# A hybrid block (linear attention, routed experts, state-space scan) in fp32: a third buffer of transposed rows, convolution products moved into the batch ahead, and a new slot table

## Chip, cores, metric

One core of one Trainium2 chip runs the whole block as one program. The metric is device microseconds of one execution, lower is better. The engines are TensorE (PE, its weight loads PEld), VectorE (DVE), ScalarE (ACT), GpSimd (POOL) and SyncE (SP, which here only issues DMAs).

## What is computed

`x` has 8 sequences ("batches") of 512 rows of 256 floats. Three residual blocks follow each other, each on a layer-normalised input:

```
x = x + attention(norm(x))      # 16 heads, linear: feature map elu+1
x = x + experts(norm(x))        # router, top 1 of 8, 256 -> 512 -> 256
x = x + ssm(norm(x))
ssm: xz = x @ in_proj.T;  xc, z = split(xz)           # 512 channels each
     u  = causal conv over 4 taps, full 512 x 512 channels, + bias
     dt = clip(sigmoid(u @ dt_w.T + dt_b));  B, C = u @ B_w.T, u @ C_w.T
     for t: state = exp(-dt*exp(A_log)) * state + dt*B*u + 1e-6   # 16 states
            y = sum_n(state * C) + D*u
     out = (y * silu(z)) @ out_w.T
x = x + experts(norm(x))        # the same experts again
```

The line above shows the order of the calls in the kernel: attention, experts, state-space block, experts.

## The kernel before

Everything is fp32 and stays in SBUF where it fits: 128 partitions, x as 32 chunks of 128 rows. The program has five stages: attention over the 8 batches (to about 210 us), experts (to about 395 us), a preparation for the scan (to 462 us), the scan stage (to 1254 us), experts again. Every engine has its own instruction list, and they wait for each other by counting semaphores.

**The scan stage** takes most of the time. Each batch is 64 **slots**, q = 0 to 63: state n = q // 4 of the 16 states, channel block k = q % 4 of the four blocks of 128 channels. In every slot

- ACT makes the decay `exp(dt*a)` of three slots later into one of five tiles (`m_decay`, L781) and one 128 x 512 quarter of the scaled input of the next state (`m_input`, L791);
- PE turns the scaled input from time-major to channel-major by four transposes into one of three PSUM banks (`m_spread`, L1366, which is the line of the helper `turned` for all transposes of this kind);
- DVE runs the recurrence over 512 times as one scan instruction (`m_scan`, L1241), which needs the decay and the bank.

After the four scans of a state POOL multiplies the 128 x 2048 result by that state's row of C (`c_product`, L530; SP has broadcast the row from DRAM into one of two tiles, L417), and adds it by an accumulating DMA onto the state two before (`add_on`, L539): two chains, of even and of odd states. States 0 and 1 start the chains. One ring of seven tiles (`m_h`) holds the scanned states; two of the seven lie in the upper half of `x`.

Between these fixed parts hangs all the other work, and **the table of slot numbers** at the top of the file tells in which slot of its engine each piece stands; it is the order within each engine's list and no clock time. For the *next* batch: 32 convolution products on PE (`m_conv`, L1668, at `CONV_AT`: four outputs of eight products), copy of u out of PSUM on ACT (`UC_AT`, L729), its transposes (`UT_AT`, L1676), B and C (`BC_AT`, L1685), dt (`DT_AT`, L1699), its tanh, clip and transposes, the weighing with dt on DVE (`WT_AT`). For the batch in hand: the gate z (`Z_AT`, L1730, and `ZTH_AT`, `GATE_AT`, L1183). For the batch *before*: skip terms on ACT (`SKIP_AT`, L772), sums of the two chains on DVE (`ADD_AT`, L1191 and L1198), the product with the gate (`FINAL_AT`, L1203), output products (`OUT_AT`, L1741), the update of x (`UPDATE_AT`, L1212) and row statistics. For the batch *after the next*: the norm of its rows on POOL (`m_norm`, L523, behind the products of the states in `NORM_AFTER`), its transposes on PE (`XT_AT`) and their copy on ACT into one of two buffers `m_xt` (`m_xtcopy`, L723, at `XTC_AT`). At slots 59, 61 and 62 PE also multiplies constants into a bank that nobody reads (`m_spin`, L1802).

The norm writes two chunks at a time into `m_xn`, which shares its memory with `m_bc` (B and C of the next batch), and so waits until C is stored. x keeps four batches of rows in its lower half; SP loads a later batch's rows into a freed place once, at state 2 of batches 2 to 5.

The last batch has no successor; PE instead turns the finished rows of the other batches for the second router (`x_turn`). Rows of the first four batches are fetched back from DRAM into `staged` (L442) for that. POOL leaves the last state's product to DVE (`m_last_product`, L1248).

**Attention** is a loop over batches; the first one stands apart. In it DVE takes the row statistics of all batches from 2 on (L875) and the scales (L882 to L895) between its work on k and the mask of kv (L969, L970), which PE needs for the attention product (L1404). ACT's first activation (L573) loads its function table.

## Time and profile before

| what | value |
|---|---|
| median of 3 runs | 1473.14 us (1471.19 to 1476.2) |
| the profiled execution | 1464.08 us, span 1462.3 us, mean granted PE clock 0.975 |
| PE busy | 1363.0 us, 93% of the span |
| DVE busy | 1017.6 us, 70% |
| ACT busy | 934.8 us, 64% |
| POOL busy | 868.0 us, 59% |
| DMA | 248.39 MB, mean 170 GB/s |

"Busy" is the time in which an engine had an instruction in work; matmuls are pipelined, so PE's figure also holds time in which the next one could have started but did not. The granted clock is 1.00 at TensorE's 2.4 GHz and 0.50 at its 1.2 GHz. A row of windows has its bounds and length, then busy us and number of instructions of PE, PEld, DVE, ACT and POOL, then the granted clock (mean), the DMA engines' mean busy share and GB/s. A row of a timeline has start, length (first start to last end), engine, line, operation, output and inputs, how many in a row, and in brackets the idle time ahead and what ended it. The order's rows further down name the instruction, its output and inputs, and how often it stands in a row; a 512-column matmul is one such row and two records in the trace.

### The profile page before, as it was taken

What the parts mean: (1) busy time and instruction counts of PE and PEld (TensorE: products, weight loads), DVE (VectorE), ACT (ScalarE), POOL (GpSimd) and SP (SyncE); (2) the same over time, 40 slices, a digit from 0 to 9 for tenths busy, and PEclk for the clock granted to TensorE, in tenths of its full rate; (3) what the DMA queues carried; (4) which work ended last, traced back from release to release, by engine and by line L of the source; (5) the groups of instructions that cost most, each with busy time, mean ns of one, the idle gap of its engine ahead of it and who ended that gap; (6) DMA issues with size and microseconds to landing.
All of it is one profiled execution on the core that took longest, in us unless ns stands there. A gap on an engine that the chain in (4) does not pass through costs nothing.

```text
span 1462.3 us, 22311 instructions
## 1 busy us (share of the span) xinstructions
PE 1363.0 (93%) x7072; PEld 959.2 (66%) x7072; DVE 1017.6 (70%) x1535; ACT 934.8 (64%) x1735; POOL 868.0 (59%) x440
## 2 busy tenths in 40 slices
PE   5899997999999999999999999999999788889997
PEld 2566686999764555565655655656556576569996
DVE  6666635333344899899898998998998988853332
ACT  1222232344326999999998998999999998114442
POOL 1110002555211898898898898988988878325552
PEclk9999999999999999999999999999999978999999
DMA  9400014766420797998997988989979978376662
GB/s 297 162 29 27 17 31 145 212 207 209 151 70 23 168 219 176 197 220 183 202 224 178 213 191 193 222 188 198 224 165 206 240 188 194 83 237 211 207 208 80
DMA packets 108229, 248.39 MB, mean 170 GB/s; under 512 B 19097, under 2 KB 49950, under 8 KB 94048
## 3 DMA queue, kind: packets, MB, share of 16 engines
q0 software_dynamic: 23104, 131.96, 41.7%
q1 hardware_dynamic: 82944, 113.68, 25.6%
q10 hardware_dynamic: 2080, 1.47, 0.3%
q8 instruction: 55, 0.90, 0.3%
q14 instruction: 46, 0.38, 0.1%
HBM read 116.72 MB, written 18.94 MB: 93 GB/s over the span
## 4 chain that ended last, share of the span: by engine, by line
PE 68%; ACT 17%; DVE 9%; issue 4%; DMA 2%; POOL 0%; DVEq 0%; POOLq 0%; ACTq 0%; SPq 0%
PE ps L1366 11%; PE ps L1579 10%; PE ps L1588 9%; ACT arena L781 7%; PE ps L1699 7%; ACT arena L791 7%; PE ps L1668 5%; PE ps L1391 4%; PE ps L1741 3%; PE ps L1730 3%; DVE arena L1241 2%; PE ps L1428 2%; PE ps L1685 2%; PE ps L1382 2%; PE ps L1497 2%
## 5 line engine op out<-in xcount | busy, mean ns | idle before, releaser
L530 POOL TENSOR_TENSOR arena<-arena 128x2048 f32<-128x2048 f32 x91 | 424.9, 4685 | 107.3 <-DVE arena L1241 102.6
L1366 PEld LDWEIGHTS ps<-cst,arena 128*128 128x128 f32 x2428 | 299.7, 145 | 279.3 <-issue 190.9
L1241 DVE TENSOR_TENSOR_SCAN arena<-arena,ps 128x512 f32<-128x512 f32 x364 | 431.9, 1210 | 62.4 <-PE ps L1366 55.0
L1366 PE MATMUL ps<-cst,arena 128*128 128x128 f32 x2428 | 370.4, 281 | 50.3 <-ACT arena L791 23.8
L781 ACT ACTIVATE arena<-arena,a_neg 128x512 f32<-128x512 f32 x512 | 366.1, 715 | 40.7 <-DVE arena L1241 30.0
L791 ACT ACTIVATE arena<-arena,m_bt 128x512 f32<-128x512 f32 x510 | 361.8, 710 | 2.0 <-PE ps L1366 1.1
L1668 PE MATMUL ps<-arena,tapw 128*128 128x512 f32 x448 | 224.5, 595 | 0.0
L1241 DVE TENSOR_TENSOR_SCAN x<-arena,ps 128x512 f32<-128x512 f32 x148 | 175.6, 1209 | 19.8 <-PE ps L1366 18.4
L530 POOL TENSOR_TENSOR x<-x,arena 128x2048 f32<-128x2048 f32 x36 | 170.1, 4734 | 13.4 <-DVE x L1241 13.2
L1114 DVE TENSOR_TENSOR arena<-ps,arena 128x256 f32<-128x256 f32 x78 | 33.2, 425 | 201.5 <-PE ps L1588 195.9
L477 POOL DMA_INDIRECT arena<-rows,arena x78 | 75.7, 971 | 157.6 <-DVE arena L1094 134.4
L1579 PEld LDWEIGHTS ps<-arena 128*128 128x128 f32 x1248 | 154.8, 196 | 3.8
L1579 PE MATMUL ps<-arena 128*128 128x128 f32 x1248 | 155.1, 279 | 0.0
L1588 PE MATMUL ps<-arena 128*128 x624 | 147.5, 380 | 0.0
L667 ACT ACTIVATE arena<-ps 128x256 f32<-128x256 f32 x78 | 29.9, 383 | 159.4 <-PE ps L1366 159.4
L1699 PE MATMUL ps<-arena,dtw 128*128 128x512 f32 x256 | 128.8, 597 | 0.6 <-ACT arena L729 0.6
L1588 PEld LDWEIGHTS ps<-arena 128*128 128x128 f32 x624 | 112.6, 190 | 12.4
L674 ACT ACTIVATE arena<-ps,b1t 128x128 f32<-128x128 f32 x312 | 89.0, 368 | 41.3 <-issue 31.8
L468 POOL TENSOR_TENSOR x<-x,arena 128x1024 f32 (+1 forms) x8 | 18.8, 2351 | 120.4 <-DVE arena L904 115.1
L1668 PEld LDWEIGHTS ps<-arena,tapw 128*128 128x128 f32 x448 | 72.5, 191 | 18.0 <-issue 16.8
L492 POOL DMA_INDIRECT out_x<-arena x39 | 39.3, 1008 | 66.5 <-DVE arena L1121 66.5
L492 POOL DMA_INDIRECT residual<-arena x39 | 39.4, 1010 | 66.1 <-DVE arena L1121 66.1
(173 smaller groups left out, 1628.8 us busy)
## 6 DMA issues: line engine op xcount, KB each, us to landing
arena<-arena POOLq DMA_DIRECT2D x52, 1024.0 KB, 8.3
arena<-in_W SPq DMA_DIRECT2D x94, 512.0 KB, 4.3
arena<-c_rows SPq DMA_DIRECT2D x128, 256.0 KB, 3.7
arena<-x POOLq DMA_DIRECT2D x28, 1024.0 KB, 8.4
x<-arena POOLq DMA_DIRECT2D x24, 1024.0 KB, 8.2
rows<-x SPq DMA_DIRECT2D x16, 512.0 KB, 4.3
x<-residual SPq DMA_DIRECT2D x12, 512.0 KB, 5.9
x<-in_x SPq DMA_DIRECT2D x8, 512.0 KB, 11.2
```

Of the source, the lines that this page charges most:

```text
L477: g.indirect_dma_start(out=t_x[j % XB], out_offset=None, in_=xs[r], in_offset=bass.IndirectOffsetOnAxis(ap=idx[:, j:j + 1], axis=0))\
L492: g.indirect_dma_start(out=x_mid if r == 0 else T["out"].rearrange("b s d -> (b s) d"), out_offset=bass.IndirectOffsetOnAxis(ap=idx[:, j:j ...
L530: g.tensor_tensor(h, h, m_c[i % RC].unsqueeze(1).to_broadcast([P, KI, SEQ]), ALU.mult)\
L674: last = a.activation(t_ht[par][:, k, :], ps[4 + par][:, k * P:(k + 1) * P], ACT.Relu, bias=b1t[:, row(e), k:k + 1].rearrange("p a b -> p ...
L781: a.activation(m_a[g % RA], m_dt[b % 2][:, k, :], ACT.Exp, scale=a_neg[:, k, n:n + 1])\
L791: a.activation(m_dbt[i % 2][:, c, :], m_wt[b % 2][:, c, :], ACT.Copy, bias=1e-6, scale=m_bt[b % 2][:, c, n:n + 1]).then_inc(S("m_dbt"), 1)
L1241: v.tensor_tensor_scan(out=h[:, k, :], data0=m_a[g % RA], data1=ps[SCAN_BANK[g % 3]][:, :], initial=0.0, op0=ALU.mult, op1=ALU.add).then_i ...
L1366: return t.transpose(bank, src[:, k * P:(k + 1) * P], ident)
L1579: last = t.matmul(ps[4 + par][:, h * P:(h + 1) * P], t_w1[j % WR][:, k, h * P:(h + 1) * P], t_xt[par][:, k, :], start=(k == 0), stop=(k == ...
L1588: last = t.matmul(ps[6 + par][:, 0:D], t_ht[par][:, k, :], w2[:, row(e), k, :].rearrange("p a h -> p (a h)"), start=(k == 0), stop=(k == K ...
L1668: mm = t.matmul(ps[CONV_BANK[o]][:, :], tapw[:, k, d, o * P:(o + 1) * P], m_xt[n % 2][:, d, k:k + SEQ], start=(i == 0), stop=(i == TAPS * ...
L1699: mm = t.matmul(dt_bank(n, o)[:, :], dtw[:, k, o * P:(o + 1) * P], m_u[n % 2][:, k, :], start=(k == 0), stop=(k == KI - 1))
```

## The change

- A **third buffer of turned rows** `m_xt[2]`, and `m_xn` in its own place, both in the part of `x` that held the rows of batches 2 and 3. The norm no longer waits for the store of C, but for the transposes of the batch before.
- So x keeps fewer rows: chunks 0 to 3 for the batch that is finished, 4 to 7 for the one that is normalised. Rows are **loaded twice** by SP, once for the norm (at state 5, `N_LOAD`) and once for the update (at state 2). Batches 4 and 5 are fetched back for the router too, into `tapw`, at state 14 of batch 6, and the rows of the last batch with them.
- The **first five convolution products** of output block 0 for batch b + 2 stand in slots 59 to 63 of batch b. For batch 1 they stand in slot 0 of batch 0.
- **No constant products** at the end of a batch.
- A **new slot table** for nearly all pieces.
- The row of C of the second to last state has a tile of its own (`c_last`), loaded at state 12 of the last batch.
- In the first attention batch, the statistics are spread: two behind each of the four kv biases, five ahead of the mask, three and the scales behind it. PE turns the first batch's rows chunk by chunk, and ACT runs a small exponential ahead of its first wait.

```diff
@@ -48,40 +48,41 @@
...
-XN = 2
+XN, XTS = 2, 3
...
-CONV_AT = ((0, 1, 2, 2, 3, 4, 5, 6), (7, 8, 8, 10, 11, 12, 13, 14), (14, 15, 16, 17, 18, 20, 21, 21), (22, 23, 24, 26, 28, 29, 30, 30))
...
-SPIN_AT = (59, 61, 62)
-C_STORE = 10
...
-NORM_AFTER = (9, 10, 11, 12)
...
+CONV_AT = ((-5, -4, -3, -2, -1, 0, 1, 2), (2, 2, 3, 4, 5, 6, 7, 8), (10, 11, 12, 12, 13, 14, 15, 16), (17, 18, 18, 19, 20, 21, 22, 23))
...
+SPIN_AT = ()
+C_STORE = 14
+N_LOAD = 5
...
+NORM_AFTER = (6, 9, 10, 11)
...
@@ -97,7 +98,7 @@
-EARLY = 8
+EARLY, LATE = 8, 3
@@ -270,6 +271,9 @@
...
         m_xt = [s.take(KD * (SEQ + PAD)).rearrange("p (k t) -> p k t", k=KD) for _ in range(2)]
+        freed = x[:, 2 * CPB:4 * CPB, :].rearrange("p c d -> p (c d)")
+        m_xt.append(freed[:, 0:KD * (SEQ + PAD)].rearrange("p (k t) -> p k t", k=KD))
+        m_xn = freed[:, 3 * SEQ:3 * SEQ + XN * D].rearrange("p (c d) -> p c d", c=XN)
         m_wt = [s.take(CPB * DI).rearrange("p (c d) -> p c d", c=CPB) for _ in range(2)]
...
@@ -284,15 +288,18 @@
...
         m_bc = s.take(SEQ)
-        m_xn = m_bc.rearrange("p (c d) -> p c d", c=XN)
+        xn_first = m_bc.rearrange("p (c d) -> p c d", c=XN)
...
                   for w in (m_dt[0].rearrange("p k t -> p (k t)"), u_raw[0]) for i in range(2)]
+        staged += [tapw[:, k].rearrange("p d n -> p (d n)").rearrange("p (c d) -> p c d", c=CPB) for k in range(2)]
         x_turned = ([f_xt[i % 2] for i in range(BATCH)], [halves[i // IN_LAST][i % 2] for i in range(BATCH)])
...
         c_end = u_raw[0][:, 0:SEQ]
+        c_last = m_xt[BATCH % 2][:, 0, 0:SEQ]
...
@@ -306,7 +313,11 @@
...
-            return CPB * (b % RING)
+            return CPB if b == BATCH - 1 else 0
+        def rows_in(n):
+            return CPB if n else 0
...
@@ -420,21 +433,38 @@
...
                         store_rows(1, b - 1)
-                    if n == 2 and 2 <= b < BATCH - 2:
-                        new = b + RING - 2
+                    if n == 2 and b >= 2:
                         sp.wait_ge(S("f1_rows"), 16 * (b - 1))
                         if b > 2:
-                            sp.wait_ge(S("ld_again"), 16 * (b - 2))
-                        sp.dma_start(x[:, kept(new):kept(new) + CPB, :],
-                                     x_mid[new * SEQ:(new + 1) * SEQ].rearrange("(c p) d -> p c d", p=P))\
-                            .then_inc(S("ld_again"), 16)
+                            sp.wait_ge(S("ld_late"), 16 * (b - 2))
+                        sp.dma_start(x[:, 0:CPB, :], x_mid[(b - 1) * SEQ:b * SEQ].rearrange("(c p) d -> p c d", p=P))\
+                            .then_inc(S("ld_late"), 16)
+                    if n == N_LOAD and b < BATCH - 2:
+                        sp.wait_ge(S("m_xn"), CPB * (b + 2))
+                        if b:
+                            sp.wait_ge(S("ld_rows"), 16 * b)
+                        sp.dma_start(x[:, CPB:2 * CPB, :],
+                                     x_mid[(b + 2) * SEQ:(b + 3) * SEQ].rearrange("(c p) d -> p c d", p=P))\
+                            .then_inc(S("ld_rows"), 16)
+                    if n == NS - 2 and b == BATCH - 2:
+                        sp.wait_ge(S("m_umm"), KI * BATCH)
+                        sp.wait_ge(S("f1_rows"), 16 * (BATCH - 2))
+                        for k in range(RING, BATCH - 2):
+                            sp.dma_start(staged[k], xs[1][k * SEQ:(k + 1) * SEQ, 0:D].rearrange("(c p) d -> p c d", p=P))\
+                                .then_inc(S("ld_back0"), 16)
+                        sp.wait_ge(S("m_xn"), NCH)
+                        sp.wait_ge(S("ld_rows"), 16 * (BATCH - 2))
+                        sp.dma_start(x[:, CPB:2 * CPB, :], x_mid[(BATCH - 1) * SEQ:BATCH * SEQ].rearrange("(c p) d -> p c d", p=P))\
+                            .then_inc(S("ld_rows"), 16)
                     if b == BATCH - 1 and n == NS - 4:
                         sp.wait_ge(S("f_tr"), BATCH + FEED_ORDER[1].index(2) + 1)
+                        sp.wait_ge(S("m_zmm"), KI * (BATCH - 1))
+                        sp.dma_start(c_last, c_rows[b % 2][NS - 2].partition_broadcast(P)).then_inc(S("m_c_end"), 16)
                         sp.dma_start(c_end, c_rows[b % 2][NS - 1].partition_broadcast(P)).then_inc(S("m_c_end"), 16)
-                    if b == BATCH - 1 and n == NS - 2:
-                        break
                     if b == BATCH - 1 and n in BACK_AT:
                         k = BACK_AT.index(n)
+                        if k == 0:
+                            sp.wait_ge(S("ld_back0"), 32)
                         sp.wait_ge(S("f1_rows"), 16 * RING)
...
@@ -510,24 +543,28 @@
...
                                 m_xt[0][:, :, PAD:PAD + SEQ - 1:2], ALU.subtract).then_inc(S("m_xd"), 1)
+            g.wait_ge(S("m_stat0"), 2)
+            g.memset(m_xt[2][:, :, 0:PAD], 0.0).then_inc(S("m_zero"), 1)
...
                 if c == 0:
-                    g.wait_ge(S("m_cst"), 16 * n)
-                    g.wait_ge(S("m_btr"), n)
-                    if n >= RING:
-                        g.wait_ge(S("ld_again"), 16 * (n - RING + 1))
+                    g.wait_ge(S("m_xct"), CPB * n)
+                    g.wait_ge(S("ld_rows"), 16 * (n - 1))
                 if c >= XN:
...
                 i = CPB * n + c
-                g.tensor_scalar(m_xn[:, c % XN, :], x[:, kept(n) + c, :], rstd[:, i:i + 1], nw[2][:, i:i + 1],
+                g.tensor_scalar(m_xn[:, c % XN, :], x[:, rows_in(n) + c, :], rstd[:, i:i + 1], nw[2][:, i:i + 1],
                                 ALU.mult, ALU.add).then_inc(S("m_xn"), 1)
...
                 g.wait_ge(S("m_scan"), KI * (i + 1))
-                g.wait_ge(S(f"m_cl{i % RC}"), 16 * (i // RC + 1))
-                g.tensor_tensor(h, h, m_c[i % RC].unsqueeze(1).to_broadcast([P, KI, SEQ]), ALU.mult)\
+                last = i == NS * BATCH - 2
+                if last:
+                    g.wait_ge(S("m_c_end"), 32)
+                else:
+                    g.wait_ge(S(f"m_cl{i % RC}"), 16 * (i // RC + 1))
+                g.tensor_tensor(h, h, (c_last if last else m_c[i % RC]).unsqueeze(1).to_broadcast([P, KI, SEQ]), ALU.mult)\
                     .then_inc(S("m_cp"), 1)
...
@@ -599,6 +636,8 @@
...
+            a.wait_ge(S("set"), 2)
+            a.activation(a_nr[:, 0:HPT], zero_row[:, 0:HPT], ACT.Exp)
             a.wait_ge(S("ld_a"), 16 * 7)
...
@@ -706,21 +745,20 @@
...
                     if n:
-                        a.wait_ge(S("m_cst"), 16 * n)
-                        a.wait_ge(S("m_btr"), n)
-                    if n >= RING:
-                        a.wait_ge(S("ld_again"), 16 * (n - RING + 1))
+                        a.wait_ge(S("m_xct"), CPB * n)
                 if c >= XN:
...
                 i = CPB * n + c
-                a.activation(m_xn[:, c % XN, :], x[:, kept(n) + c, :], ACT.Identity, bias=nw[2][:, i:i + 1],
+                a.activation((m_xn if n else xn_first)[:, c % XN, :], x[:, rows_in(n) + c, :], ACT.Identity, bias=nw[2][:, i:i + 1],
                              scale=rstd[:, i:i + 1]).then_inc(S("m_xn"), 1)
...
                 a.wait_ge(S("m_xct"), CPB * (n + 1))
-                if n >= 2 and k == 0:
-                    a.wait_ge(S("m_zmm"), KI * (n - 1))
-                a.activation(m_xt[n % 2][:, k, PAD:], ps[XT_BANK[k]][:, :], ACT.Copy).then_inc(S("m_xtc"), 1)
+                if n == 2 and k == 0:
+                    a.wait_ge(S("m_zero"), 5)
+                if n >= XTS and k == 0:
+                    a.wait_ge(S("m_zmm"), KI * (n - XTS + 1))
+                a.activation(m_xt[n % XTS][:, k, PAD:], ps[XT_BANK[k]][:, :], ACT.Copy).then_inc(S("m_xtc"), 1)
...
@@ -926,6 +968,8 @@
...
                     v.tensor_tensor(a_k[:, c, :], ps[4 + c % 2][:, 0:D], bkv[:, 0:D], ALU.add).then_inc(S("a_kb"), 1)
+                    for i in rows[2 * c:2 * c + 2]:
+                        row_stats(i)
...
@@ -992,14 +1036,21 @@
...
                         row_stats(c)
-                a_kvbias(b)
+                later = range(2 * CPB + EARLY, NCH)
+                a_kvbias(b, () if before else later[0:2 * CPB])
                 a_qfeature(b)
                 a_kfeature(b)
-                if not before:
-                    first_stats(2 * CPB + EARLY, NCH, 2 * CPB)
                 if before:
                     a_update(b - 1)
+                else:
+                    for i in later[2 * CPB:-LATE]:
+                        row_stats(i)
                 a_mask(b)
+                if not before:
+                    for i in later[-LATE:-1]:
+                        row_stats(i)
+                    link(row_stats(NCH - 1))
+                    layer_norm_scales(2 * CPB, NCH)
...
@@ -1366,8 +1418,15 @@
...
+            def a_turn_first():
+                for c in range(CPB):
+                    t.wait_ge(S("a_xn0"), c + 1)
+                    for k in range(KD):
+                        last = turned(ps[k][:, c * P:(c + 1) * P], a_xn[:, c, :], k, c)
+                last.then_inc(S("a_tr"), 1)
             def a_turn(b):
-                t.wait_ge(S("a_xn"), b + 1)
+                t.wait_ge(S("a_xn"), b)
                 if not (isinstance(b, int) and b == 0):
...
@@ -1859,6 +1919,10 @@
...
                         m_prep(b + 1, q)
+                        for o in range(KI):
+                            for i in range(TAPS * KD):
+                                if b < BATCH - 2 and q - SLOTS == CONV_AT[o][i]:
+                                    m_conv(b + 2, o, i)
                         if q in SPIN_AT:
...
```

What the table does to the lists, at three places. **DVE in the first attention batch**, from the first kv bias (L926 and L928 before, L968 and L970 now) to the mask. Before:

```order
L928 TENSOR_TENSOR arena<-ps,arena 128x256
L961 SCALAR_TENSOR_TENSOR arena<-arena 128x1024
L932 TENSOR_SCALAR arena<-arena 128x1024
L934 SCALAR_TENSOR_TENSOR arena<-arena 128x1024
L875 BN_STATS stats<-x 128x6 x16
L882 TENSOR_TENSOR nw<-stats 128x24
...
L895 SCALAR_TENSOR_TENSOR scales<-nw,scales 128x24
L969 TENSOR_TENSOR arena<-ps,cst 128x128
L970 TENSOR_SCALAR arena<-cst,ps 128x8
```

and now:

```order
L970 TENSOR_TENSOR arena<-ps,arena 128x256
L913 BN_STATS stats<-x 128x6 x2
L1005 SCALAR_TENSOR_TENSOR arena<-arena 128x1024
L976 TENSOR_SCALAR arena<-arena 128x1024
L978 SCALAR_TENSOR_TENSOR arena<-arena 128x1024
L913 BN_STATS stats<-x 128x6 x5
L1013 TENSOR_TENSOR arena<-ps,cst 128x128
L1014 TENSOR_SCALAR arena<-cst,ps 128x8
L1013 TENSOR_TENSOR arena<-ps,cst 128x128
L1014 TENSOR_SCALAR arena<-cst,ps 128x8
L913 BN_STATS stats<-x 128x6 x3
L920 TENSOR_TENSOR nw<-stats 128x24
```

Of sixteen statistics in one row, five are left ahead of the mask, and the scales stand behind it.

**PE at the end of a batch**, from the last gate product (L1730 before, L1790 now) over slots 59 to 63 into slot 0 of the next. The rows of 128x128 are the transposes of the slots. Before:

```order
L1730 MATMUL ps<-arena,zw 128x512
L1802 MATMUL ps<-cst 128x512
L1366 MATMUL ps<-cst,arena 128x128 x8
L1802 MATMUL ps<-cst 128x512
L1366 MATMUL ps<-cst,arena 128x128 x4
L1802 MATMUL ps<-cst 128x512
L1366 MATMUL ps<-cst,arena 128x128 x8
L1668 MATMUL ps<-arena,tapw 128x512
```

and now (the last row here is slot 2's; L1728 is the convolution):

```order
L1790 MATMUL ps<-arena,zw 128x512
L1728 MATMUL ps<-x,tapw 128x512
L1418 MATMUL ps<-cst,arena 128x128 x4
L1728 MATMUL ps<-x,tapw 128x512
...
L1418 MATMUL ps<-cst,arena 128x128 x4
L1728 MATMUL ps<-x,tapw 128x512 x3
```

The three constant products are gone, and one convolution product stands in each of the five slots. In slot 0 of batch 0 the list now has

```order
L1418 MATMUL ps<-cst,arena 128x128 x4
L1728 MATMUL ps<-arena,tapw 128x512 x6
L1418 MATMUL ps<-cst,arena 128x128 x4
L1728 MATMUL ps<-arena,tapw 128x512
```

where one product stood between the transposes of slots 0 and 1.

**POOL from the product of state 9** (L530 before, L567 now; the adding DMAs L539, L576; the norms L523, L556). Before:

```order
L530 TENSOR_TENSOR arena<-arena 128x2048
L523 ISA
L523 TENSOR_SCALAR arena<-x,scales,nw 128x256
L539 DMA arena<-arena 128x2048
L530 TENSOR_TENSOR x<-x,arena 128x2048
L523 TENSOR_SCALAR arena<-x,scales,nw 128x256
L539 DMA arena<-x 128x2048
L530 TENSOR_TENSOR x<-x,arena 128x2048
L523 TENSOR_SCALAR arena<-x,scales,nw 128x256
L539 DMA arena<-x 128x2048
```

and now:

```order
L567 TENSOR_TENSOR arena<-arena 128x2048
L556 TENSOR_SCALAR x<-x,scales,nw 128x256
L576 DMA arena<-arena 128x2048
L567 TENSOR_TENSOR x<-x,arena 128x2048
L556 TENSOR_SCALAR x<-x,scales,nw 128x256
L576 DMA arena<-x 128x2048
L567 TENSOR_TENSOR x<-x,arena 128x2048
L556 TENSOR_SCALAR x<-x,scales,nw 128x256
L576 DMA arena<-x 128x2048
L567 TENSOR_TENSOR arena<-arena 128x2048
```

The first norm went to state 6; the second to fourth follow states 9, 10 and 11, each a state earlier than before, and the third is the first that needs a transpose of its own batch to be done.

## Rows read from the trace of the kernel before

**Rows 1.** Windows over batches 0, 6 and 7.

```profile
462.50:555.80 93.30, 90.14 (x427) 52.88 (x426) 81.87 (x78) 89.89 (x147) 80.99 (x31) 1.00 0.78 172
1054.20:1153.60 99.40, 95.42 (x455) 57.99 (x454) 90.82 (x97) 92.59 (x151) 86.03 (x32) 1.00 0.90 198
1153.60:1253.60 100.00, 83.99 (x480) 67.16 (x480) 84.77 (x87) 86.05 (x149) 79.89 (x27) 0.83 0.84 195
```

**Rows 2.** Windows, batch 3: slots 0-11, 12-19, 20-47, 48-63.

```profile
755.30:772.20 16.90, 16.16 (x76) 9.32 (x75) 15.83 (x17) 16.90 (x29) 15.39 (x5) 1.00 0.95 220
772.20:785.90 13.70, 12.77 (x59) 7.14 (x58) 13.70 (x18) 12.05 (x20) 10.84 (x4) 1.00 0.57 133
785.90:829.90 44.00, 44.00 (x214) 27.69 (x213) 37.12 (x38) 40.10 (x65) 38.19 (x16) 1.00 0.94 203
829.90:854.90 25.00, 23.48 (x116) 14.55 (x115) 24.22 (x28) 24.31 (x41) 22.65 (x10) 1.00 0.98 221
```

**Rows 3.** The chain in batch 3: start, length, engine, line; pieces of one kind.

```profile
759.21 0.58 ACT ps L772
...
761.05 0.61 ACT arena L781
...
784.10 0.97 PE ps L1685 x2
...
794.57 0.87 PE ps L1741 x4
...
804.78 0.87 PE ps L1366 x8
...
806.96 0.86 PE ps L1699 x2
```

**Rows 4.** Timeline and chain, DVE in batch 3.

```profile
838.08 2.32 DVE L1241 TENSOR_TENSOR_SCAN arena<-arena,ps 128x512 f32<-128x512 f32 x2
...
776.84 1.19 DVE ps L1198 x2
```

**Rows 5.** Waits of batch 3: us in total, times, longest.

```profile
PE ps L1676 <- ACT arena L729: 0.9, 1, 0.9
```

**Rows 6.** Timeline of the first attention batches.

```profile
14.29 1.28 ACT L573 ACT_TABLE_LOAD   x1 [14.14 <-PE ps L1366]
...
34.04 5.31 DVE L875 BATCH_NORM_STATS2 stats<-x 128x6 f32<-128x256 f32 x16
...
43.77 3.99 PE L1404 MATMUL ps<-arena 128*128 128x136 f32 x16 [4.10 <-DVE arena L970]
...
47.92 0.35 DVE L943 TENSOR_SCALAR arena<-ps 128x24 f32<-128x24 f32 x3 [3.11 <-PE ps L1404]
```

**Rows 7.** Timeline at the end of the scan stage.

```profile
1251.41 4.51 POOL L530 TENSOR_TENSOR arena<-arena 128x2048 f32<-128x2048 f32 x1 [2.85 <-DMA arena<-c_rows]
...
1253.85 4.43 DVE L1248 TENSOR_TENSOR x<-x,arena 128x512 f32<-128x512 f32 x4
```

**Rows 8.** DMA issues with time to landing: two windows of batch 7, one of batch 3.

```profile
arena<-rows SPq DMA_DIRECT2D x1, 512.0 KB, 16.2
...
arena<-c_rows SPq DMA_DIRECT2D x1, 256.0 KB, 15.0
...
arena<-x POOLq DMA_DIRECT2D x1, 1024.0 KB, 11.1
...
rows<-x SPq DMA_DIRECT2D x1, 512.0 KB, 4.7
```

**Rows 9.** Timeline of POOL, batch 3, and a landing at the same place.

```profile
837.12 0.55 POOL L523 TENSOR_SCALAR arena<-x,scales,nw 128x256 f32<-128x256 f32 x1 [1.96 <-PE ps L1366]
...
855.26 0.87 POOL L539 DMA_DIRECT2D arena<-x  x1 [0.37 <-POOL x L530]
...
arena<-x POOLq DMA_DIRECT2D x1, 1024.0 KB, 9.4
```

**Rows 10.** Windows: ten us of batch 7.

```profile
1160.00:1170.00 10.00, 7.70 (x44) 7.18 (x44) 7.71 (x9) 10.00 (x19) 8.33 (x2) 0.66 1.01 254
```

85 lines of the change are left out of this document (48 added, 37 removed).

## The prediction

> **What bounds the kernel now.** I read the busy times by batch of the scan stage first [rows 1]: eight batches of 64 slots take about 790 of the 1462.3 us (462.5 to 1253.6), and in a batch like the sixth PE, ACT and DVE are busy for 95.42, 92.59 and 90.82 of 99.40 us. Batch 3, cut in four by the starts of its scans, tells who sets the pace where [rows 2]: slots 0 to 11 ACT (16.90 of 16.90 us), slots 12 to 19 DVE, where the closing additions of the batch before lie (13.70 of 13.70), slots 20 to 47 PE (44.00 of 44.00), slots 48 to 63 nobody fully (ACT 24.31, DVE 24.22 of 25.00). The batch takes 99.6 us.
>
> Prices per instruction, as steps on the chain, where work is back to back: a decay or an input scaling on ACT 0.61, another ACT operation 0.58, a 512-column matmul 0.86 (two records), four transposes 0.44, a 32-row one 0.97, a pair of 256-column records 0.43 [rows 3]; a scan 1.11 (2.32 for two, less the last one's 1.21), another DVE operation 0.59 [rows 4].
>
> Counting the table of before with them: ACT 128 x 0.61 and 23 x 0.58, 91.7 us a batch; DVE 64 scans and 26 others and some small ones, 88.6; PE 94.5, of which the three constant products 2.6. So 5 to 11 us of each engine go in handing over. The longest PE wait that I can name is for ACT's u (0.9) [rows 5].
>
> **The change, a steady batch (1 to 6).** I add the stretches in which one engine binds.
>
> Slots 48 to 63 and 0 to 11, ACT: before 28 slots of 1.22 and 11 single operations, 40.7 of work, in 25.0 + 16.9 = 41.9 us. The new table has 13 single ones there (two evacuations of u come early), 41.8. The gates now stand three slots and more from the z products that wait for them, so I allow 0.4 of loss where there was 1.2: 42.2. The constant products and five convolution products change places under this cover: PE has 19.5 us of work in slots 48 to 63 now, where 22.6 stood, and gains nothing by it directly.
>
> Slots 12 to 19, DVE: eight scans and nine others (eight before), 9.0 + 5.3 = 14.2, where 13.7 was measured.
>
> Slots 20 to 47, PE: 28 groups of four transposes 12.2, 4 convolution products 3.5, 16 of dt 13.8, 16 output products 6.9, 4 of B and C 3.9, 5 transposed blocks 2.2 and B's turn 0.4: 42.9. Before it was 43.2 and took 44.0: PE had stood for u just ahead (its evacuation is at ACT's slot 18, its transposition at 19 [rows 5]) and entered with no lead. Now these two stand at 16 and 20, and from slot 48 to 19 PE has 49.0 us of work beside the 56.4 of the other two stretches. Three product banks let it run two whole slots ahead, 3.0 us at its price for slots 20 and 21, of which I take back 1.9 for waits inside (the update at slot 31 stands before the output product at 32 that it needs): 41.8.
>
> Sum 98.2. One more row load of 512 KB a batch: batch 6, which has none, takes 99.4, against 99.6 for those with one [rows 1, 2], so 0.2. **98.4 us, 1.2 less; six batches: -7.2.** Bounds: below, the largest engine's own work of 91.9 (PE) with 4.6 for handing over, 96.5; above, no lead and the longer DVE and ACT stretches, 44.0 + 14.2 + 42.3 = 100.5.
>
> **Batch 0.** Its convolution products for batch 1 have no batch ahead; five more stand in slot 0, as the order shows: 5 x 0.86 = 4.3 us before scan 1's input. Some returns, since later slots of this ACT-bound batch (93.3 us [rows 1]) have fewer. +3.4, between +1 and +5.
>
> **The start.** DVE takes 16 row statistics and the scales between its last kv operation and the mask; PE waits 4.10 for it, from 39.7 to 43.77 [rows 6]. Of the 16, eight go into gaps of the kv bias, five stay (1.7 us) and three and the scales (0.33 each; 3.4 for the scales: 39.35, where the statistics end, to 43.77 is 4.4, the mask and the handover about 1.0 of it) come behind the mask. PE can attend near 37.3, 6.5 earlier; but DVE then normalises at about 43.2 where it did at 47.92, so what moves is 4.8. The table load of 1.28 on ACT goes where ACT is idle, 1.2. Together -6.0 (-5 to -7.5).
>
> **The last batch.** (a) At the end product 126 waited for its row of C until 1251.41 and then ran beside DVE's own four products, which took 4.43 [rows 7] against 4 x 0.59 = 2.4. Its row now comes four states earlier into its own tile, so it starts when product 125 ends, 2.85 earlier: -2.0 (0 to -2.3). (b) Behind state 14 of batch 6 SP now issues two staged batches and one of rows, 1.5 MB, while the adding DMAs run. Staged rows beside them took 16.2 us, and the row of C behind them 15.0 where a store took 4.7 alone beside them [rows 8]. Row 15 of C is wanted 12.5 us after those loads; if it lands 20 behind, POOL is 7 late, and DVE's additions of the odd chain at slot 12 have some 2 to 4 us of room. I take +3, between -2 (POOL idles anyway in this batch) and +7.
>
> **Sum**: -7.2 + 3.4 - 6.0 - 2.0 + 3.0 = -8.8. The profiled execution (1464.1 us, span 1462.3) would be 1455.3; it lay 9 us under the median of the runs, 1473.14, to which I apply the same difference: **1464.3 us**, 0.6% faster. About 0.3% (4.4 us) is what a measurement can tell from no change.
>
> **The rivals.**
>
> *More than that (0.14).* The table and the third buffer pay in full and a batch falls to some 95.7: 3.9 x 6 = 23 us, so 1448. For it: each engine's own work is under 92. Against: stretches in which one engine is full make three quarters of the batch [rows 2], and the new table keeps the nine DVE operations together.
>
> *Nothing gained in a batch (0.12).* The early convolution products wait for ACT's copies at slots 58 and 62, PE enters slot 20 without lead; 99.8 a batch. Then +1.2 + 3.4 - 6.0 - 2.0 + 3.0 = -0.4: 1472.7.
>
> *Slower: POOL's third norm (0.15).* It stands behind product 10 now, ahead of that product's adding DMA, and needs the transposes of slot 50; before it stood behind product 11, waited 1.96 us for slot 52, and the last even adding DMA went out at 855.26, 0.3 us into the next batch [rows 9]. Now a whole product, its issue and a gap (6.0) come after the wait, which ends 2 slots (2.9 us) earlier: 3.1 later at least, 4.6 if slots 48 to 63 go faster. With 9.4 to land [rows 9] the even chain is summed 12.8 to 14.3 us into the batch. DVE's two first additions stand at slot 7, at 12.5 (eight ACT slots of 1.22 and five single operations); ACT, two slots ahead, absorbs some 0.7, so at 9.4 the loss is 0 to 1.1. It decides if landings grow: the adding DMAs took 11.1 in batch 7 [rows 8], and slots 48 to 63 already have a DMA share of 0.98 [rows 2], into which the same bytes are to go in less time. Then both chains are up to 2.8 late, right before DVE's own stretch, where nothing is made up: 101.2 a batch, +9.6 + 3.4 - 6.0 - 2.0 + 3.0 = +8.0, 1481.
>
> *The burst of loads costs ten (0.07)*: 1471.3.
>
> *The clock (0.09).* Without constant products slots 52 to 54 hold almost only transposes, some 2 us of PE work in 4.3. In batch 7, where PE has little but transposes, the granted clock was 0.66 over ten us, and 0.83 over the batch [rows 1, 10], that is 1.2 GHz at times; a batch with the constant products had 1.00. A drop like that one, 6.8 of ten us at the lower level, once a batch costs 3.4 of PE's work, half of it under ACT's cover: 6 x 1.7 = 10 us, 1474.5. The Trainium skill (TensorE: Matmul & The Clock Gate, Part 4: PE-mode transpose) says that transposes do not count as activity of TensorE as other matmuls do; by that rule this drop would come in each batch and the time be this rival's. Batch 7 agrees with it in part only: a mean of 0.83 is the full clock for two thirds of the time, on little but transposes.
>
> **How the numbers follow.** My forecast has 0.41, with its own range of 1456 to 1470. Faster by over 0.3%: nearly all of that and the first rival, 0.57. Within: the second, the burst, the clock, the forecast's upper edge, 0.24. Slower: the POOL rival and the upper ends together, 0.19. The remaining 0.02 is burst and POOL at once. The range leaves a tenth at either side: 1450 to 1481.
>
> **What would show it.** A batch of 98 to 99 us; in slots 20 to 47 PE still full and the stretch at 42 us, with no wait of PE for u; DVE at slots 12 to 19 full for 14.2; batch 0 near 97; the first attention products at 37.5 instead of 43.77; DVE's last four products at 2.4 us. The POOL rival would show as DVE idle before the line of the even additions, for a DMA; the burst as POOL idle for a row of C at the seam of batches 6 and 7; the clock as a granted clock under 1.00 in batches 1 to 6. I am wrong in the main step if the batch stays at 99.6 or falls under 97.

## The result, and the profile after

The changed kernel is slower: a median of 1492.43 us (1481.03 to 1501.13) against 1473.04, a ratio of 1.0138 with a 95% interval of 1.0097 to 1.0179. The profiled execution took 1481.03 us (span 1479.2), 16.95 more than the one of before. I had forecast 1464.3, between 1450 and 1481. Here and below a ratio leaves out executions more than 1.5% above the fastest of the same kernel: one of 3543 us in e0_again, one of twelve in e5_norm11, four in e8_start_clast, two in e12_conv, four of the kernel before.

The page of the kernel after (busy time, then the chain that ended last):

```profile
PE 1349.9 (91%) x7030; PEld 944.4 (64%) x7030; DVE 1013.5 (69%) x1535; ACT 928.3 (63%) x1736; POOL 867.3 (59%) x441
...
PE 56%; issue 10%; DMA 9%; ACT 9%; POOL 8%; DVE 6%; another core or an unknown queue 1%; ACTq 0%; SPq 0%; DVEq 0%; POOLq 0%
```

PE is busy for 13 us less than before, and its share of the chain fell from 68 to 56%: POOL and the DMAs, which held 0 and 2% before, hold 8 and 9%.

Windows over batches 0, 3, 5, 6 and 7, as in [rows 1]:

```profile
461.90:557.70 95.80, 90.85 (x428) 52.78 (x427) 82.09 (x77) 89.45 (x147) 76.63 (x31) 1.00 0.72 161
758.60:858.40 99.80, 94.98 (x453) 56.72 (x452) 90.47 (x97) 92.45 (x152) 86.93 (x35) 1.00 0.90 206
958.50:1060.40 101.90, 96.16 (x453) 57.61 (x452) 90.62 (x96) 92.36 (x152) 86.39 (x34) 0.98 0.89 202
1060.40:1161.00 100.60, 90.26 (x442) 54.70 (x440) 90.42 (x97) 92.00 (x151) 89.56 (x31) 1.00 0.93 208
1161.00:1273.10 112.10, 81.70 (x479) 66.06 (x478) 85.23 (x87) 85.87 (x148) 83.48 (x30) 0.83 0.85 198
```

Laid against my sum, in the two profiled executions:

| part | forecast | measured |
|---|---|---|
| start, up to the first scan | -6.0 | -0.6 (462.5 to 461.9) |
| batch 0 | +3.4 | +2.5 |
| batches 1 to 6 | -7.2 | +5.5 (597.8 to 603.3) |
| batch 7 | +3.0 | +12.1 |
| behind the last batch | -2.0 | -2.6 (208.7 to 206.1) |

**A steady batch.** Batch 3, slots 0-3, 4-7, 8-11, 12-19, 20-47 and 48-63 (the cuts of [rows 2], the first stretch in three):

```profile
758.60:765.40 6.80, 6.80 (x29) 3.83 (x28) 4.85 (x6) 6.50 (x12) 6.50 (x3) 1.00 1.00 224
765.40:773.40 8.00, 8.00 (x40) 4.72 (x38) 6.03 (x6) 8.00 (x14) 7.70 (x3) 1.00 1.05 242
773.40:778.50 5.10, 2.88 (x16) 1.81 (x16) 5.10 (x7) 4.24 (x7) 5.00 (x2) 1.00 0.94 237
778.50:793.00 14.50, 14.50 (x65) 8.19 (x64) 14.43 (x18) 13.07 (x21) 11.99 (x5) 1.00 0.62 147
793.00:835.60 42.60, 42.33 (x207) 25.90 (x206) 37.77 (x40) 38.39 (x64) 36.89 (x15) 1.00 0.98 219
835.60:858.40 22.80, 20.47 (x102) 12.26 (x101) 22.29 (x26) 22.25 (x38) 18.83 (x10) 1.00 0.85 193
```

Slots 48 to 63 fell from 25.0 to 22.8 and slots 20 to 47 from 44.0 to 42.6: that is the table's gain. It goes again in slots 0 to 11, which take 19.9 us where they took 16.9, and 0.8 more goes in slots 12 to 19. In slots 4 to 7 DVE is busy 6.03 of 8.00 us; this stretch is the one that differs from batch to batch (7.9, 9.4, 8.0, 8.4, 9.5 and 9.3 us in batches 1 to 6; slots 12 to 19 of batch 5 add 0.7). What DVE waits for in batch 5, as us in total, times and longest, and POOL around the norms and at the seam of batches 3 and 4:

```profile
DVE ps L1242 <- DMA arena<-arena: 2.8, 1, 2.8
```

```profile
829.79 4.84 POOL L567 TENSOR_TENSOR arena<-arena 128x2048 f32<-128x2048 f32 x1
838.82 0.55 POOL L556 TENSOR_SCALAR x<-x,scales,nw 128x256 f32<-128x256 f32 x1 [4.18 <-PE ps L1418]
839.35 0.88 POOL L576 DMA_DIRECT2D arena<-arena  x1
...
862.77 0.87 POOL L576 DMA_DIRECT2D arena<-x  x1 [0.37 <-POOL x L567]
```

The third norm stands behind product 10 and waits 4.18 us for a transpose of PE's slot 50. The last even adding DMA goes out at 862.77, 4.4 us into the next batch, where it was 0.4 [rows 9]; 4.0 of slack went, and DVE's additions at slot 7 now wait for it, 1.1 to 2.8 us in batches 1 to 6. The adding DMAs for which they wait in batches 2 to 5 took 10.8, 9.5, 9.6 and 11.0 us to land.

**The last batch.** PE and POOL at its start, then the landings of the three loads in the order of their issue (KB each, us from issue to landing), then four pieces of the chain that ended last:

```profile
1159.72 1.53 PE L1418 MATMUL ps<-cst,arena 128*128 128x128 f32 x12 [2.80 <-ACT arena L829]
1173.99 1.97 PE L1418 MATMUL ps<-cst,tapw 128*128 128x128 f32 x8 [12.74 <-DMA tapw<-rows]
```

```profile
1176.16 4.54 POOL L567 TENSOR_TENSOR arena<-arena 128x2048 f32<-128x2048 f32 x1 [14.25 <-DMA arena<-c_rows]
```

```profile
tapw<-rows SPq DMA_DIRECT2D x1, 512.0 KB, 9.0
tapw<-rows SPq DMA_DIRECT2D x1, 512.0 KB, 19.9
x<-residual SPq DMA_DIRECT2D x1, 512.0 KB, 19.8
```

```profile
1156.98 19.05 DMA arena<-c_rows
...
1176.17 4.54 POOL arena L567
...
1181.08 10.96 DMA x<-arena
...
1192.06 0.71 DVE ps L1249
```

At slot 2 of batch 7 PE turns the rows of batch 4, which SP asked for at 1153.68, 7.6 us before; it stands 12.74 us, and behind it in its list stand the transposes of all further slots. The rows of batch 4 had landed after 9.0 us, at 1162.7, when PE had waited 1.4 us. But both fetches count on one semaphore, and PE waits for the sum of both (`ld_back0`, 32), so for the rows of batch 5, which it does not read here: they landed at 1174.0.

POOL is held as well, and the chain runs through it and not through PE. SP issued the loads only when the store of batch 5's rows had landed, and the row of C for state 15 behind them, at 1156.98. It landed at 1176.03; POOL had been ready since 1161.91 and stood 14.25 us. Its product's adding DMA then landed at 1192.04, and DVE, which PE had already held for 12.46 us, waited another 1.67 us for it at slot 12. That addition starts 31.1 us into the batch, where it started 18.9 us into it before. So two paths from the same loads end within 2 us of each other, POOL's the later.

**Start and end.** The first attention batch of after, then the chain at the end of attention, after and before, then DVE's last four products:

```profile
33.14 1.73 DVE L913 BATCH_NORM_STATS2 stats<-x 128x6 f32<-128x256 f32 x5
...
42.29 0.35 DVE L987 TENSOR_SCALAR arena<-ps 128x24 f32<-128x24 f32 x3
```

```profile
186.89 6.08 PE ps L1487 x16
```

```profile
192.83 3.56 PE ps L1428 x16
```

```profile
1273.16 2.50 DVE L1299 TENSOR_TENSOR x<-x,arena 128x512 f32<-128x512 f32 x4
```

DVE normalises at 42.29 instead of 47.92 [rows 6]. At the end of attention the kernel is 6.8 us ahead (its last L1463 products start at 177.29, those of L1404 before at 184.05), but 16 matmuls behind them take 6.08 us instead of 3.56: the granted clock was 0.50 from 186 to 190 us, where it had been 1.00. At the first gather (238.2 us) 1.8 of the lead was left, and when the experts' first products ran it was gone: those 2.4 us went behind the gather, where the chain waits 5.28 us for a queue that it cannot name and the clock was 0.50 from 242 to 246 us, so that their cause is not shown. DVE's last products take 2.50 instead of 4.43 [rows 7].

### The profile page after: what moved, and what is told of

The parts are those of the page before. It is cut to its first block, busy times and chain, and to the rows that moved or that the text cites. A ratio compares the mean times of both kernels' runs of the same rounds, so it can differ in the third digit from the quotient of the medians.

```text
span 1479.2 us, 22253 instructions
## 1 busy us (share of the span) xinstructions
PE 1349.9 (91%) x7030; PEld 944.4 (64%) x7030; DVE 1013.5 (69%) x1535; ACT 928.3 (63%) x1736; POOL 867.3 (59%) x441
## 4 chain that ended last, share of the span: by engine, by line
PE 56%; issue 10%; DMA 9%; ACT 9%; POOL 8%; DVE 6%; another core or an unknown queue 1%; ACTq 0%; SPq 0%; DVEq 0%; POOLq 0%
PE ps L1647 9%; PE ps L1638 9%; PE ps L1418 8%; PE ps L1728 6%; POOL arena L567 4%; PE ps L1450 4%; ACT arena L819 3%; ACT arena L829 3%; PE ps L1759 3%; DMA arena<-c_rows 3%; PE ps L1487 2%; DVE arena L1292 2%; DMA arena<-arena 2%; PE ps L1441 2%; PE ps L1556 2%
## 5 line engine op out<-in xcount | busy, mean ns | idle before, releaser
L567 POOL TENSOR_TENSOR arena<-arena 128x2048 f32<-128x2048 f32 x91 | 428.9, 4721 | 92.9 <-DVE arena L1292 56.3
L1418 PEld LDWEIGHTS ps<-cst,arena 128*128 128x128 f32 x2372 | 289.4, 145 | 293.0 <-issue 163.5
L1292 DVE TENSOR_TENSOR_SCAN arena<-arena,ps 128x512 f32<-128x512 f32 x364 | 427.4, 1206 | 65.9 <-PE ps L1418 59.1
L1418 PE MATMUL ps<-cst,arena 128*128 128x128 f32 x2372 | 365.2, 281 | 69.1 <-ACT arena L829 29.0
L567 POOL TENSOR_TENSOR x<-x,arena 128x2048 f32<-128x2048 f32 x36 | 171.0, 4760 | 16.0 <-DMA arena<-c_rows 8.9
L1728 PE MATMUL ps<-arena,tapw 128*128 128x512 f32 x320 | 160.8, 597 | 0.4
L501 POOL TENSOR_TENSOR x<-x,arena 128x1024 f32 (+1 forms) x8 | 18.9, 2357 | 114.4 <-DVE arena L942 108.9
L1801 PE MATMUL ps<-outw,arena 128*128 128x256 f32 x224 | 66.4, 384 | 0.0
```

Source lines behind the costliest of these rows:

```text
L567: g.tensor_tensor(h, h, (c_last if last else m_c[i % RC]).unsqueeze(1).to_broadcast([P, KI, SEQ]), ALU.mult)\
L1292: v.tensor_tensor_scan(out=h[:, k, :], data0=m_a[g % RA], data1=ps[SCAN_BANK[g % 3]][:, :], initial=0.0, op0=ALU.mult, op1=ALU.add).then_i ...
L1418: return t.transpose(bank, src[:, k * P:(k + 1) * P], ident)
L1728: mm = t.matmul(ps[CONV_BANK[o]][:, :], tapw[:, k, d, o * P:(o + 1) * P], m_xt[n % XTS][:, d, k:k + SEQ], start=(i == 0), stop=(i == TAPS ...
```

## Experiments

Each ratio is to the kernel before, timed on the same chip, with its 95% interval. The runs stand on five chips, so two runs of one chip compare more closely than two of different ones.

| run | edit against | ratio |
|---|---|---|
| e0_again | the changed kernel itself | 1.0135 (1.0095 to 1.0174) |
| e1_norm | changed | 1.0193 (1.0158 to 1.0228) |
| e2_burst | changed | 1.0048 (1.0007 to 1.0090) |
| e4_spin | changed | 1.0112 (1.0081 to 1.0142) |
| e5_norm11 | changed | 1.0030 (1.0000 to 1.0059) |
| e6_norm11_burst | changed | 1.0000 (0.9971 to 1.0029) |
| e7_norm11_burst_spin | e6 | 1.0069 (1.0034 to 1.0104) |
| e8_start_clast | before | 0.9976 (0.9939 to 1.0012) |
| e9_nostart | changed | 1.0096 (1.0063 to 1.0130) |
| e10_bcc | e6 | 1.0007 (0.9975 to 1.0039) |
| e11_bcc_nostart | e10 | 0.9965 (0.9939 to 0.9991) |
| e12_conv | e11 | 0.9985 (0.9961 to 1.0010) |
| e13_start | before | 1.0029 (0.9994 to 1.0064) |
| e14_conv_start | e12 | 1.0000 (0.9963 to 1.0038) |
| e15_conv_again | e12 itself | 0.9978 (0.9950 to 1.0007) |

### The changed kernel again (e0_again)

> The changed kernel unaltered, to see how its own executions differ. It was 1492.4 us in the median of four, from 1481.0 to 1501.1, and the two longest had a mean granted clock of 0.958 against 0.973 and 0.971. Theory A (late landings): the clock is a side effect; executions differ because DVE's additions at slot 7 and PE's transposes of fetched rows wait for DMAs whose landing varies; then a profile of a long execution shows longer waits there and the clock at 1.00 in batches 1 to 6. Theory B (the clock): a long execution shows granted clocks well under 1.00 in batches 1 to 6, with PE work of 1.7 us or more lost each time. Both expect a median of 1485 to 1500.

The five executions that count have a mean of 1485.5 us and a median of 1481.5. The profile is like the first: batches 99.1 to 101.4 at a granted clock of 1.00 from batch 1 to 5, batch 7 111.1. The executions at 1491.7 and 1496.1 us had a mean clock of 0.959 and 0.956; their profiles were not kept, so this run does not tell A from B. In the long executions of other kernels below the low clock stands ahead of the scan stage and not in batches 1 to 6, where B had put it.

### The norm one state later (e1_norm)

```diff
-NORM_AFTER = (6, 9, 10, 11)
+NORM_AFTER = (6, 9, 11, 12)
```

> Third and fourth norm moved one state later (behind products 11 and 12). Theory A (POOL's third norm): POOL's wait of 4.2 us behind product 10 goes, the last even adding DMA is issued some 3 us earlier, DVE's wait at slot 7 (1.4 to 2.9 us in the profile) goes, slots 4 to 7 take 6.5 instead of 8.1 to 9.6, a batch 98.3: 6 x 2.1 = 12 us off, so about 1480. Rival (a landing that is late for its own reasons, the traffic at the seam): slots 4 to 7 stay over 8 us and the time within 3 us of the changed kernel's. Rival (the fourth norm, now behind product 12, holds up PE's transposes at slots 54 and 55): stretch 48 to 63 grows by 1 us or more a batch, no gain.

Windows of batch 5, slots 4-7 and 48-63, and PE's waits in it:

```profile
979.70:986.40 6.70, 6.70 (x34) 4.06 (x34) 6.00 (x7) 6.70 (x12) 5.60 (x2) 1.00 0.97 220
...
1048.90:1076.80 27.90, 23.16 (x103) 14.22 (x102) 22.51 (x26) 23.03 (x39) 24.61 (x13) 0.88 1.01 229
```

```profile
PE ps L1418 <- POOL x L556: 4.7, 2, 4.2
```

The first theory was right of its stretch: slots 4 to 7 take 6.65 us in every batch from 1 to 6, and DVE's wait is gone. But the last rival held too, and by more than I had said: PE waits 4.2 us for the fourth norm where it had 1.4, and in five of the batches 0 to 5 the clock fell in slots 48 to 63, which took 24.7 to 27.9 us. The time rose to a median of 1493.1 us, where the first theory had about 1480.

### Both late norms behind product 11 (e5_norm11)

```diff
-NORM_AFTER = (6, 9, 10, 11)
+NORM_AFTER = (6, 9, 11, 11)
```

> Third and fourth norm both behind product 11. In e1_norm the wait at slot 7 went (slots 4 to 7 took 6.65 where they took 8.1 to 9.6), but the fourth norm came late, PE waited 3.4 us a batch for it where it had waited 1.4, and the clock fell in slots 48 to 63 of five batches. Theory A (the idle of PE ahead of slot 55 brings the clock down): here the third norm is 1.2 us later than in the changed kernel and the fourth 4 us earlier, PE waits at most 2.6 us, the clock in slots 48 to 63 stays at 1.00 in most batches, slots 4 to 7 stay at 6.65, batches of 98.5 to 99, and the median is 1478 to 1484. Theory B (the clock falls by chance in any version without constant products): drops in slots 48 to 63 as in e1_norm, median 1486 to 1495.

Batch 3, slots 4-7, 48-63 and the whole, and POOL in it:

```profile
779.00:785.60 6.60, 6.60 (x33) 3.98 (x32) 5.93 (x6) 6.60 (x12) 6.30 (x3) 1.00 1.04 226
...
848.20:870.90 22.70, 20.16 (x102) 12.36 (x101) 22.19 (x25) 22.16 (x38) 21.95 (x10) 1.00 1.02 235
```

```profile
772.20:870.90 98.70, 94.41 (x453) 56.95 (x452) 90.53 (x96) 92.15 (x152) 89.35 (x35) 1.00 0.93 209
```

```profile
852.72 1.34 POOL L556 TENSOR_SCALAR x<-x,scales,nw 128x256 f32<-128x256 f32 x2
853.76 1.13 POOL L576 DMA_DIRECT2D arena<-arena  x1
...
871.48 0.87 POOL L576 DMA_DIRECT2D arena<-x  x1 [0.37 <-POOL x L567]
```

POOL waits for no transpose, the last even adding DMA goes out 0.6 us into the next batch, and batches 2 to 5 take 98.7 us each, within 0.1 of each other. The median, 1475.4 against 1469.9, stands 1.05% of before lower than that of the changed kernel (1.0030 after 1.0135, on another chip). Theory A held in its mechanism: one number in the table stands for 1.8 us a batch (98.7 instead of 100.5), 11 us in all. The median came out under its range of 1478 to 1484; 1.05% are 15 us, but the two intervals, from two chips, leave that uncertain by about 7.

### The fetches taken apart (e2_burst, e6_norm11_burst)

```diff
-                    if n == NS - 2 and b == BATCH - 2:
+                    if n in (8, NS - 2) and b == BATCH - 2:
+                        k = RING + (n != 8)
                         sp.wait_ge(S("m_umm"), KI * BATCH)
-                        sp.wait_ge(S("f1_rows"), 16 * (BATCH - 2))
-                        for k in range(RING, BATCH - 2):
-                            sp.dma_start(staged[k], xs[1][k * SEQ:(k + 1) * SEQ, 0:D].rearrange("(c p) d -> p c d", p=P))\
-                                .then_inc(S("ld_back0"), 16)
-                        sp.wait_ge(S("m_xn"), NCH)
-                        sp.wait_ge(S("ld_rows"), 16 * (BATCH - 2))
-                        sp.dma_start(x[:, CPB:2 * CPB, :], x_mid[(BATCH - 1) * SEQ:BATCH * SEQ].rearrange("(c p) d -> p c d", p=P))\
-                            .then_inc(S("ld_rows"), 16)
+                        sp.wait_ge(S("f1_rows"), 16 * (k + 1))
+                        sp.dma_start(staged[k], xs[1][k * SEQ:(k + 1) * SEQ, 0:D].rearrange("(c p) d -> p c d", p=P))\
+                            .then_inc(S("ld_rows" if n == 8 else "ld_back0"), 16)
```

(The waits of PE and DVE on these loads are counted to match.)

> Batch 4 is fetched back at state 8 of batch 6, batch 5 alone at state 14, and the rows of batch 7, which still lie in place from their norm, are not loaded a second time. Theory A (the burst holds PE): the wait of 12.7 us of PE for the fetched rows at slot 2 of batch 7 goes, and with it nearly all of what the last batch is longer by: batch 7 at 100 to 101 us instead of 112.2, 11 to 12 us off, so about 1481. Rival (the row of C behind the loads, as I forecast): POOL still waits over 5 us for its row at the seam and batch 7 stays over 105.

> The same norms with the loads of e2_burst. The two losses are independent by both theories, so the median is that of e5_norm11 less 11 to 13 us: 1466 to 1472 by theory A, 1474 to 1483 by theory B. If the two are one loss told twice, it stays within 4 us of e2_burst's 1474.1.

Batch 7 of e2_burst, and PE at its start:

```profile
1158.10:1256.20 98.10, 81.63 (x481) 67.18 (x480) 85.25 (x87) 85.91 (x148) 83.46 (x30) 0.86 0.92 215
```

```profile
1158.79 1.91 PE L1414 MATMUL ps<-cst,tapw 128*128 128x128 f32 x8
```

The transposes of the fetched rows wait for nothing, the batch takes 98.1 instead of 112.1 us, and the ratio falls from 1.0135 to 1.0048 on one chip, 12.7 us between the means. The run takes away the burst whole, and with it PE's wait and POOL's (0.66 us for its row of C at the seam here, where it had 14.25), one of the three loads, and the shared semaphore. It does not tell these apart: by the chain above, PE's wait taken away alone would have gained nothing, and POOL's alone at most the 1.7 us by which it ended later (an estimate from those rows).

With the norms of e5_norm11 the time is that of before, 1466.6 against 1469.9: no longer slower, and no faster. That median is 8.8 us under that of e5_norm11, where 11 to 13 were expected (the ratios, 1.0030 and 1.0000, are 4 apart); batch 7 took 102.9 us in this profile, with the clock at 0.73 to 0.89 up to slot 55.

### The constant products back (e4_spin, e7_norm11_burst_spin)

```diff
-SPIN_AT = ()
+SPIN_AT = (59, 61, 62)
```

> The three constant products back at slots 59, 61 and 62, all else as changed. Theory B (the clock): the granted clock over batches 1 to 6 rises to 1.00 throughout, all executions have a mean clock near 0.973, the long ones vanish and the median falls from 1492 to about 1482. Theory A: 2.6 us of PE work a batch are added where ACT sets the pace; the time stays within 4 us of the changed kernel's or grows by 0 to 6, and the executions spread as before.

> As e6_norm11_burst, with the three constant products back at slots 59, 61 and 62. By theory A they cost 0 to 1 us a batch, since the clock stayed up already: 1466 to 1476. By theory B they hold the clock: 5 to 12 us less than e6_norm11_burst and a narrower spread of the executions.

Slots 48-63 of batch 3 in e7_norm11_burst_spin:

```profile
841.90:866.20 24.30, 22.40 (x109) 13.75 (x108) 22.48 (x26) 23.16 (x39) 20.69 (x11) 1.00 1.03 234
```

With the early convolution products in the same slots the constant ones are not under ACT's cover: the stretch takes 24.3 us instead of 22.8, the batch 100.0 instead of 98.7, and the median is 13 us over e6_norm11_burst's, 3.6 us more than theory A allowed. In e4_spin, where the late norm takes its toll anyway, the mean was 3.3 us under that of e0_again, with intervals that overlap. In batches 1 to 6 the clock was 1.00 in these two profiles; without the products it was too, but for one batch in each of the two profiles of the changed kernel (0.98 in batch 5 above; 0.92 and 0.93 in parts of batch 6 of e0_again). And with them it fell as well, to 0.79 in slots 48 to 55 of batch 0 of e7. Theory B falls for the scan stage: it is not the missing constant products that the time went with.

### Later copies of B and C (e10_bcc), one product moved (e12_conv)

```diff
-BT_AT = 31
-BCC_AT = 30
-BTC_AT = 31
+BT_AT = 33
+BCC_AT = 32
+BTC_AT = 34
```

> e6_norm11_burst with ACT's copy of B and C two slots later (32), PE's turn of B at 33 and DVE's copy of it at 34. In all profiles with the new table slots 28 to 31 take 8.78 us (6.75 before) and ACT stands 1.94 us at its slot 30 for PE's last product of B and C, which is PE's slot 30 too. Theory A (that wait is on the path): slots 28 to 31 take 6.7 to 7.2 and the batch 96.8 to 97.2 where it was 98.7; 7 x 1.7 = 12 us off, ratio to before 0.992. Rival (PE is full there anyway and the time comes back in slots 32 to 47): these rise from 22.85 to over 24 and the batch stays over 98.2, ratio 0.998 to 1.000.

Slots 28-31 and 32-47 of batch 3, in e6_norm11_burst and then in e10_bcc:

```profile
800.80:809.60 8.80, 8.80 (x38) 4.68 (x38) 5.71 (x6) 6.84 (x12) 6.48 (x5) 1.00 0.86 197
809.60:832.40 22.80, 22.54 (x117) 15.11 (x116) 22.70 (x26) 21.15 (x35) 21.54 (x9) 1.00 1.02 221
```

```profile
814.40:822.70 8.30, 8.30 (x35) 4.46 (x34) 5.47 (x5) 6.88 (x12) 4.53 (x2) 1.00 0.86 192
822.70:846.20 23.50, 22.99 (x121) 15.42 (x120) 22.89 (x27) 21.68 (x36) 22.83 (x11) 1.00 0.95 209
```

The rival held: the batch stayed at 98.8 us and the ratio at 1.0007, though slots 32 to 47 rose only to 23.5 us and not over 24. ACT's wait went and nothing was won: PE is full in the first stretch and nearly so in the second, and 0.5 us saved in one is 0.7 spent in the other.

```diff
-CONV_AT = ((-5, -4, -3, -2, -1, 0, 1, 2), (2, 2, 3, 4, 5, 6, 7, 8), (10, 11, 12, 12, 13, 14, 15, 16), (17, 18, 18, 19, 20, 21, 22, 23))
+CONV_AT = ((-5, -4, -3, -2, -1, 0, 1, 2), (2, 3, 4, 4, 5, 6, 7, 8), (10, 11, 12, 12, 13, 14, 15, 16), (17, 18, 18, 19, 20, 21, 22, 23))
```

> e11_bcc_nostart with one convolution product moved from slot 2 to slot 4 (three stood at slot 2, behind five slots with one each). In all profiles with the new table slots 0 to 3 take 6.80 us, 1.5 more than before, with DVE idle 1.9 us at slot 2 for PE's transposes. Theory A (the cluster is the cause): slots 0 to 3 take 5.9 to 6.3 and slots 4 to 7 at most 0.3 more, the batch 98.2 to 98.6 where it is 98.9; ratio to before 0.993 to 0.996. Rival (PE's total from slot 59 to slot 8 is the limit, 20.4 us against ACT's 20.1 by the prices of the prediction): the time comes back in slots 4 to 11 and the batch stays within 0.2 of 98.9; ratio unchanged at 0.9965.

Slots 0-3 and 4-7 of batch 3 in e12_conv:

```profile
773.30:779.30 6.00, 6.00 (x27) 3.46 (x26) 4.91 (x6) 6.00 (x11) 5.70 (x3) 1.00 1.04 233
779.30:786.80 7.50, 7.50 (x36) 4.43 (x35) 5.97 (x7) 7.50 (x13) 6.81 (x4) 1.00 1.02 223
```

Between the two: 0.8 won in slots 0 to 3 and as much spent in slots 4 to 7, as the rival said, but 0.3 won in slots 12 to 19 and the batch 98.5 instead of 98.9, as theory A had it. Too little for the median, which came out 0.2% over e11's on another chip, with three long executions among its twelve.

### The start (e8_start_clast, e13_start, e9_nostart, e11_bcc_nostart, e14_conv_start, e15_conv_again)

e8 and e13 put the diff's parts on the first attention batch into the kernel before (e8 with `c_last` too); e9 and e11 take them out of the changed kernel and of e10; e14 and e15 are one kernel with and without them.

> The kernel before with two parts of the change alone: the statistics spread in the first attention batch (with the turn of the first rows chunk by chunk and the early exponential), and the row of C of the second to last state in its own tile. My prediction's terms: -6.0 and -2.0, so 1456.5 where the kernel before takes 1464.5. Rival (given back): the start is gained but the stages behind it start at another phase of the clock and of the DMAs, as in the changed kernel's trace, where 6.8 us gained at 186 us had shrunk to 1.8 at 240 us and was gone at 252 us; then 1461 to 1465.

> The changed kernel with the first attention batch as before (statistics, scales, turn of the first rows and no early exponential). In all seven profiles with the new start the granted clock was 0.74 to 0.85 at 180 to 200 us, where the kernel before had 1.00, and in three of them it stayed near 0.50 from there to 220 us, which put the first gather at 251 to 254 us instead of 238 to 241; five of twelve executions of e8_start_clast were over 1479 us. Theory A (the new start brings the stage behind attention to a phase with a lower clock): 180 to 200 us has 1.00 again, executions 14 us over the others become rare, and the median is the changed kernel's 1.0135 of before or up to 0.5% under it although 5 to 7 us of work come back. Theory B (the long executions have nothing to do with the start): the median is 5 to 7 us over the changed kernel's (1.0175), the long ones as frequent as before.

> e10_bcc with the first attention batch as before. Theory A: the executions spread less than those of e10_bcc and none is 14 us over the rest; median within 4 us of e10_bcc's. Theory B: 5 to 7 us over it.

> The kernel before with the new first attention batch alone. Five profiles so far (e1_norm, e5_norm11, e8_start_clast, e10_bcc with the new start, e12_conv with the old one) had the granted clock near 0.50 from about 200 to 230 us and the scan stage 8 to 15 us late; the other eight of the changed kernel and its variants had not, nor had the kernel before. Theory A (the new start makes this more frequent): of twelve executions four or more are over 1476 us, of the kernel before on the same chip at most one in eight; the undisturbed ones are 6 us under before's. Theory B (it comes by chance with either start): the share is the same, the undisturbed ones are 6 us under, and the ratio is 0.996.

> e12_conv with the new first attention batch. Theory A: two or more executions of twelve 12 us or more over the fastest than e15_conv_again has, median at or over its. Theory B: as many in both, the fastest 5 to 6 us under the fastest of e15_conv_again (which had 1456.0), median as much under it, ratio 0.993 to 0.996.

> e12_conv unaltered, on the chip of the other two, for the share of executions with the low clock at 200 to 230 us (three of twelve were 12 us or more over the rest) and for the steady batch of 98.5 us: ratio to before 0.995 to 0.9985.

Windows 200-210 and 220-230 us of e14_conv_start, then of e15_conv_again:

```profile
200.00:210.00 10.00, 10.00 (x43) 8.86 (x42) 0.97 (x6) 2.37 (x5) 0.00 (x0) 0.50 0.21 9
...
220.00:230.00 10.00, 10.00 (x43) 9.21 (x42) 0.84 (x2) 1.48 (x4) 0.00 (x0) 0.50 0.01 2
```

```profile
200.00:210.00 10.00, 10.00 (x78) 8.71 (x77) 1.10 (x6) 3.85 (x9) 0.00 (x0) 1.00 0.23 13
...
220.00:230.00 10.00, 7.13 (x30) 4.75 (x28) 8.53 (x18) 1.69 (x5) 0.00 (x0) 0.91 0.32 105
```

In the first, PE is full for 30 us at 1.2 GHz, does 43 matmuls in ten of them where it did 78, and the first gather starts at 254.9 instead of 240.2 us. This event stands in seven profiles (e1, e5, e8, e10, e12, e13, e14), all of executions with a mean clock of 0.966 or less; of the executions that were only timed I count those (without e1_norm, whose clock falls in the scan stage too). With the new start they were 33 of 100, with the old one 15 of 151, and more with the new one on each chip that had both:

| chip | new start | old start |
|---|---|---|
| e0, e2, e4 | 6 of 17 | 0 of 11 |
| e5 to e8 | 9 of 43 | 4 of 30 |
| e9 to e11 | 5 of 12 | 4 of 40 |
| e12 | none | 3 of 29 |
| e13 to e15 | 11 of 24 | 4 of 41 |
| the changed kernel's first four | 2 of 4 | not recorded |

So the new start makes the event more frequent, from one execution in ten to one in three, as theory A said; e12 shows it without (3 of 12), and e5 to e7, with the new start, had only 4 of 31, so the number itself is uncertain. One part of e9's theory A did not hold: the lower clock between 185 and 190 us, 1.00 with the old start in e9 and before, was 0.76 and 0.72 in e11 and e15, which have the old start too.

The other executions show little of the gain of 6 us: their median is 1464.5 in e13 against 1465.9 of before, 1461.5 in e14 against 1463.2 in e15, 1462.8 in e10 against 1462.9 in e11. Only e8, which has `c_last` as well, was 6.2 under (1462.8 against 1469.0), of 8 forecast. Over all executions the mean with the new start was 4 to 5 us longer in the first three pairs and 0.7 in the last. Taken out of the changed kernel, the start makes it no slower (1.0096 after 1.0135, intervals that overlap).

**e11_bcc_nostart**, without the new start, with the norm and the fetches mended (and the later copies, which bring nothing), is the only version whose interval lies below 1: 0.9965 (0.9939 to 0.9991), medians 1462.9 against 1466.1. It is the best of fifteen runs, and the same kernel with one product moved came out at 0.9985 and 0.9978 with intervals that reach 1, so 0.35% is likely more than the true gain.

## Why the prediction was wrong

The sign was wrong. My sum was -8.8 and 16.9 came; of the 25.7 between them 12.7 lie in batches 1 to 6, 9.1 in the last batch and 5.4 in the start, less 1.5 in batch 0 and the tail.

- **POOL's third norm** is the step that failed first: the forecast's batch of 98.4 puts DVE's wait for the late even addition at nothing, and leaves it to a rival with 0.15. The rival was right in mechanism and nearly in size. I had said 3.1 to 4.6 us later, it was 4.0; the additions at slot 7 then wait 1.1 to 2.8 us, the batch takes 100.5 on average where the rival had 101.2, and e5_norm11 takes it away. My reason for the low chance was a landing of 9.4 us, by which the loss was 0 to 1.1; I wrote that it decides if landings grow, and they did, to 9.5 to 11.0 in batches 2 to 5.
- **The burst of loads**, term (b) of the last batch: I took +3, and +10 as a rival with 0.07. Measured +12, and e2_burst gives it back whole. The mechanism that I named, loads, row of C, POOL, odd chain, DVE, is what the chain shows; what failed is its size. "Row 15 of C is wanted 12.5 us after those loads": it was wanted 8.2 us after them, because SP issued them only when a store had landed, and it came 22.3 us after them where I had 20. So POOL was 14.25 us late and not 7, and the addition 12.2 us late, which is a room of 2.0 us where I had 2 to 4. I also did not ask who waits for the loads themselves: PE does, for 12.74 us, and by a semaphore that counts both fetches; by the rows of batch 7 that wait alone would have cost nearly as much. One of the three loads was for rows that still lay in place.
- **The +17 that one can add up is luck.** With the POOL rival at its price and the burst at 12 instead of 3 my sum gives +17.0, and 16.9 was measured; but the batches came out 4.1 us under that rival's price and the start 5.4 us over mine, and these two cancel.
- **The steady batch without that wait** came out near what was worked out: 98.7 us in e5_norm11 against 98.4. In part that is luck again, since its parts err both ways: 41.2 (forecast 42.2) in slots 48 to 11, 14.8 (14.2) in 12 to 19, 42.7 (41.8) in 20 to 47, where PE is full and enters with less lead than I gave it. e10_bcc agrees with the last: taking away what ACT waits for there won nothing.
- **The start** was right where it happens (5.6 us at DVE, 6.8 at the end of attention) and worth 0.6 at the first scan. The step that failed is the silent one, that a gain ahead of 200 us of PE-bound work keeps its size. In the profile of the changed kernel 5.0 of the 6.8 us went up to the first gather, with the granted clock at 0.50 from 186 to 190 us and at 0.66 instead of 0.86 from 210 to 220 us, and the rest behind it. The 30 us at 1.2 GHz, in about a third of the executions, come on top.
- **Batch 0** (+2.5 for +3.4) and **the tail** (4.43 to 2.50 us, -1.9 for -2.0) came out.
- **The chances** do not quite add up: the forecast's 0.41 and the first rival's 0.14 make 0.55 at most, where I wrote 0.57 for faster.
- **The clock rival** in the form I gave it, a drop once a batch for want of constant products, did not come: in the profile of the changed kernel batches 1 to 4 and 6 are at 1.00, although slots 52 to 54 hold almost only transposes. The Trainium skill (TensorE: Matmul & The Clock Gate, Part 4: PE-mode transpose) says that transposes do not count as activity as other matmuls do; in these batches no such drop shows; only batch 7, on little but transposes, is at 0.83 again, as in [rows 1]. A drop did come where PE also stood idle for up to 4.2 us ahead of them (e1_norm), in five of the batches 0 to 5; with the norms behind product 11 it came in one of these twelve batches (e5, e6). Whether the idling is its cause or only what the two have in common was not tried apart.

Left open: what brings the clock down from 200 to 230 us in some executions. Its share rises with the new start, but e12 shows it without, and no run changed the stage in which it happens. Open too: what PE's wait in the last batch and POOL's would each have cost alone, for which a run with a semaphore of its own for each fetch, or with the row of C ahead of the loads, would be needed; and why slots 0 to 3 take longer with the new table.

## What to carry to other kernels

When a transfer is moved or made larger, look for everything that it can delay: its readers on every engine with what stands behind them in their lists, and the transfers that are issued behind it with theirs. Here both paths cost about 12 us, side by side, and by the chain mending one alone would hardly have helped. Ask of each wait whether it counts more transfers than it reads. An instruction that one engine gets "for free" (a norm between two products) is a wait of that engine for another, and moving it by one place changes the slack of everything that it issues afterwards: here one number in a table was worth 11 us of 1470. A gain at the front of a kernel has to be followed to the end of the next stage before it is counted.

## What the runs showed of the hardware

- At the seam of two batches, with the adding DMAs under way, all 16 DMA engines are full (share 0.98 to 1.05). Of 1.5 MB of loads issued together there the first 512 KB landed in 9.0 us, the second and third in 19.9 and 19.8, and the 256 KB row of C behind them in 19.0, against 4.2 in the median of the execution. Taken apart over six states the two fetches had a median landing of 9.2 us (e2_burst).
- The granted clock can stay at 1.2 GHz for 30 us in which PE is busy without a gap (10.00 of 10.00 us in three windows), and it does so in some executions of a program and not in others, at the same place: 14 us of 1470 (first gather at 254.9 instead of 240.2 us), and a good part of the spread between executions.
